# A message-passing layer on one core: the near products of a group run half by half instead of alternating

## What is computed

```python
h = jnp.maximum(_layernorm(x), 0.0)
l1_s, l1_v = fctp(x_s, x_v, lin1_ws, lin1_wv, MUL)       # per node
weight = silu(silu(rbf @ fc_w1) @ fc_w2) @ fc_w3          # per edge, from its distance
gs, gv = l1_s[edge_src], l1_v[edge_src]                   # gathered rows
msg = products of weight, gs, gv and edge_sh_attr         # 256 numbers per edge
agg = segment_sum(msg, edge_dst, N) / count               # sum per destination node
l2 = agg @ lin2_w
out = x + sc + tanh(agg_s @ alpha_w) * l2
```

## Time and profile before

| what | value |
|---|---|
| median of three runs | 3177.41 us |
| span of the profiled execution, first to last instruction | 3111.8 us |
| its own time outside the span | not recorded; the median is 65.6 us above the span |
| TensorE matmuls busy | 1998.8 us (64%) |
| VectorE busy | 1672.2 us (54%) |
| GpSimd busy | 1500.1 us (48%) |
| ScalarE busy | 1094.8 us (35%) |
| mean granted TensorE clock | 0.764 of full |
| near product, line 1052 | 3126 matmuls, 472.8 us busy |

### The profile page before, as it was taken

The page is one execution under the profiler, slowest core; times in us unless marked ns, Lnnn a source line. Parts: engine busy times, 40 slices in busy tenths (PEclk is TensorE's granted clock), DMA queues, the critical chain, the costliest instruction groups (busy, mean ns, idle before and its releaser), DMA issues. The chain is left out here.

```text
span 3111.8 us, 47493 instructions
## 1 busy us (share of the span) xinstructions
PE 1998.8 (64%) x9991; PEld 1344.9 (43%) x9991; DVE 1672.2 (54%) x4467; ACT 1094.8 (35%) x3268; POOL 1500.1 (48%) x1607
## 2 busy tenths in 40 slices
PE   6566566566766666656666666665666575656567
PEld 5344344344444444434344444443444443434444
DVE  7454555455554555545455455554554554556556
ACT  6333333333333334323333233332333232334334
POOL 6544445444544444544444544544545444544452
PEclk8687777788877778777777767777877777777778
DMA  7211111121212112111111111111111111222211
GB/s 205 49 45 42 45 40 44 42 47 39 51 39 45 41 43 47 40 38 36 39 35 39 39 36 39 39 39 37 40 34 42 35 38 38 45 58 59 47 41 46
DMA packets 329818, 143.39 MB, mean 46 GB/s; under 512 B 242675, under 2 KB 304428, under 8 KB 329628
## 3 DMA queue, kind: packets, MB, share of 16 engines
q0 software_dynamic: 49344, 101.13, 12.4%
q1 hardware_dynamic: 268038, 34.58, 7.3%
q10 hardware_dynamic: 12246, 6.06, 0.7%
HBM read 127.88 MB, written 13.75 MB: 46 GB/s over the span
## 5 line engine op out<-in xcount | busy, mean ns | idle before, releaser
L990 POOL DMA_INDIRECT lin_g<-lin_table,src_ix x1542 | 1459.6, 947 | 1557.7 <-DVE w_s L1417 1017.7
L1064 PE MATMUL ps_sums<-near_sums,far_hot 128*128 128x1 f32 x520 | 119.3, 299 | 917.9 <-DVE agg L1476 842.6
L1040 PE MATMUL ps_w<-w,h 128*128 128x256 f32 x1566 | 582.8, 528 | 115.7 <-ACT h L1157 69.8
L1476 DVE SCALAR_TENSOR_TENSOR agg<-ps_sums,at_lo,agg 128x130 f32 x260 | 91.4, 352 | 893.0 <-remote 775.8
L1064 PEld LDWEIGHTS ps_sums<-near_sums,far_hot 128*128 128x128 f32 x520 | 102.0, 245 | 1082.6 <-issue 764.5
L1176 ACT ACTIVATE near_sums<-ps_near 128x257 f32<-128x257 f32 x261 | 100.7, 386 | 1168.1 <-remote 826.9
L1040 PEld LDWEIGHTS ps_w<-w,h 128*128 128x128 f32 x1566 | 423.1, 298 | 177.7 <-issue 93.0
L1168 ACT ACTIVATE lin_sh<-lin_g,harm 128x128 f32<-128x128 f32 x1563 | 483.8, 393 | 36.4 <-DMA lin_g<-lin_table 27.5
L1052 PE MATMUL ps_near<-msg,onehot 128*64 128x257 f32 x3126 | 472.8, 445 | 0.0
L1414 DVE TENSOR_TENSOR msg<-lin_sh,ps_w 128x576 f32<-128x576 f32 (+1 forms) x261 | 196.1, 751 | 455.7 <-remote 191.2
L1052 PEld LDWEIGHTS ps_near<-msg,onehot 128*64 128x64 f32 x3126 | 235.8, 162 | 234.4 <-issue 178.0
(11 more groups left out here) (175 smaller groups left out, 1983.7 us busy)
## 6 DMA issues: line engine op xcount, KB each, us to landing
lin_g<-lin_table SPq DMA_DIRECT2D x2688, 0.5 KB
lin_g<-lin_table,src_ix POOLq DMA_INDIRECT x1542
dist_in<-in_edge_weight SPq DMA_DIRECT2D x67, 96.0 KB
lin_table<-lin_out SPq DMA_DIRECT2D x24, 256.0 KB, 3.0
x_in<-in_x SPq DMA_DIRECT2D x24, 256.0 KB
xq<-in_x SPq DMA_DIRECT2D x23, 256.0 KB, 4.1
harm<-in_edge_attr SPq DMA_DIRECT2D x66, 48.0 KB
out_dram<-x_in ACTq DMA_DIRECT2D x11, 256.0 KB
```

The lines of the kernel that those rows point to most:

```text
L990: pool.indirect_dma_start(slot_tiles(s, u)[rows, t, :], None, lin_table, bass.IndirectOffsetOnAxis(ap=src_ix[rows, s.phase, u, col:col + 1 ...
L1040: mm = pe.matmul(ps_w[:, 2 * j * P:(2 * j + 2) * P], cols[:, j, :], w3[:], start=True, stop=True)
L1064: pe.matmul(ps_l2(i)[:, COUNT:COLS], far_hot[:, u, :], near_sums[:, u % 2, MSG:], start=True, stop=True)
```

## The change

In `near_layer` the two loops are exchanged. Before, the products went 0, 1, 2, 3, 4, 5 by tile, that is first half, second half, first half and so on. After, tiles 0, 2, 4 (first half) come first, then 1, 3, 5. The same six products with the same operands are issued, and the increment stays on the last one, which is tile 5 in both orders.

```diff
                             at_least(pe, near_copied, n)
                             pe.nop(nofuse=True)
-                            for j in range(PAIRS):
-                                for half in range(1 if isinstance(i, int) and i == ITERS else HALVES):
+                            for half in range(1 if isinstance(i, int) and i == ITERS else HALVES):
+                                for j in range(PAIRS):
                                     t = j * HALVES + half
                                     mm = pe.matmul(ps_near[half * NEAR:(half + 1) * NEAR, 0:MSG + 1], onehot[:, u % 2, t, :], msg[:, u % 2, t, :],
                                                    start=(j == 0), stop=(j == PAIRS - 1))
```

## The result

The changed kernel took 3197.09 us, the median of six runs (3185.86 to 3202.32). The kernel before, whose three shown runs had a median of 3177.41, took 3169.72 over six runs (3161.8 to 3177.78). The ratio is 1.0082, with a 95% interval of 1.0053 to 1.011: **slower by 0.8%, 27 us**. The forecast was slower, by 90 us, at 3267 us. Direction and range (3163 to 3390) held; the size was over three times too large.

The account below looks back on a forecast made before the run. The bound was taken to be the cycle of gather bursts and held-back TensorE completions, not matmul work. Caught sums, 72 us, plus direct payments, 18 us, make 90 us on 3177.41: 3267 us, range 3163 to 3390.

Parts of the forecast that it names:

- The bound is a cycle of bursts and holds: GpSimd gathers in unbroken bursts; TensorE's completions are held from about 4 us in until after the end; one group 10.66 us.
- If three is also the most it can pass: In TensorE's near product the second half starts with the first half's fourth matmul: nine slots, 0.69 us longer.
- Rival 1: TensorE's second half passes the whole queue, both halves overlap from the start, time stays 3177 us; chance 0.36.
- rival 2: TensorE's matmuls start only in instruction order: eleven slots, five more, 1.15 us; 3352 us; chance 0.14.
- Most near products are covered by a hold: Most near products end inside a hold, so 0.69 us more still ends before the release and costs nothing.
- 2.17 us for each sum that is caught: A segment sum held until after a burst makes the cycle 12.83 us instead of 10.66; 33 of them, 72 us.
- 26 groups pay their 0.69 directly, 18 us: Where no hold lies behind the near product, its added 0.69 us is paid directly: 26 groups, 18 us.
- Rival 3: Delayed `ps_w` is caught in a hold, joined two-group bursts are split, 88 us less, 3089 us; chance 0.09.
- Rival 4: All of the near product's added time is on the path: 179 to 364 us, 3357 to 3541; chance 0.04.

Follow-up runs that it names:

- sets 4 and 5: Two groups of runs on the same chip, some five minutes apart; the kernel before took 3176.31 us in the first (with holds), 2016.42 in the second (without).
- e1: Kernel before with the near products ordered first, first, second, first, second, second half; 2015.23 us against 2015.03, ratio 0.9999, without holds.
- e7: Kernel before, alternating order, with layer 1 moved behind the segment sum; 3136.41 us, ratio 1.0042, with holds.
- e8: Changed kernel with layer 1 moved behind the segment sum; 3179.53 us, ratio 1.0192 to the kernel before, with holds.
- sets 2 and 4: Two groups of runs with holds, each beside the kernel before, which took 3120.95 us in the first and 3176.31 in the second.
- d1: Kernel before, alternating order, with one more product of 255 columns into an unused part of the bank; 3195.3 us, ratio 1.0057, with holds.
- d3: Kernel before with all rows gathered by GpSimd and SyncE's single-row DMAs left out; 3124.06 us, ratio 0.9832, with holds.
- c1: The changed kernel itself, unedited, run again beside the kernel before; 3133.72 us, ratio 1.0038, with holds.
- e3: Kernel before, alternating order, with two more products of 255 columns into an unused part of the bank; 3175.04 us, ratio 1.0173, with holds.
- d2: The changed kernel itself, run again beside the kernel before; 3197.52 us, ratio 1.0073, with holds.
- c2_half: The changed kernel itself, run again beside the kernel before, without holds; 2013.33 us, ratio 1.0.

## Why the prediction was right in direction and wrong in size

1. *The bound is a cycle of bursts and holds, not TensorE's amount of work.* Right where the holds are: TensorE stays idle 34% of the span with 0.48 us more in each near product. But the holds come and go with the same kernel, even on one chip (sets 4 and 5). Without holds the same kernel takes 2015 us and the bound is GpSimd's issuing of gathers.
2. *"If three is also the most it can pass", three slots more, 0.69 us.* Mis-sized: the second half starts one matmul earlier, two slots, 0.48 us (2.00 against 1.52), since TensorE passes at least five waiting instructions, not three. Rival 1 (no slot lost) and rival 2 (strict order, 2.7 us) both fall. The Trainium skill (TensorE: Matmul & The Clock Gate, Part 3, "The mechanism") has matmuls start and end in strict order; the traces disagree, with 2.00 us for this order and 1.57 us for that of e1, where strict order would need three slots more in either.
3. *Most near products are covered by a hold.* Right in what follows from it: of 260 x 0.48 = 125 us added, 13, 21 and 27 us were paid in the three comparisons with the kernel before, 10 to 22%, and 43 us, 34%, between e7 and e8. That it is the holds that cover the rest was read from single groups, not tested.
4. *"2.17 us for each sum that is caught", 33 more of them, 72 us.* **This is the step that failed.** Caught sums rose by 16 (by 10 and 14 in sets 2 and 4, against the same one profile of before), not 33, and 2.17 us for each does not give the times. The 16 alone would be 35 us, above all that was measured, 27, with the direct payments still to come. e7 should have gained about 20 us and lost 15, d1 (3 more caught) should have cost 7 us and cost 19, e8 (2 more) 4 and cost 59. e7 and e8 also slowed layer 1, so the plainest case is d1; d3 (19 fewer caught, 52 us less) is the one run that the price would fit. One cycle of 12.83 us against one of 10.66 was a true reading of one place, but one cycle is not the mean. Counted over the trace, such long cycles rose by 8, and cheap one-group cycles rose by 16 beside them.
5. *26 groups pay their 0.69 directly, 18 us.* This small term was the nearest to what is seen: the price follows the near product's added length. Within set 4, 0.43 us cost 19 us and 0.48 cost 21; in set 2 the 0.48 us of c1 cost 13 and the 0.85 of e3 cost 54. That is 17%, 17%, 10% and 24% of the length added over 260 groups, so the share isn't constant, and with more length it seems to grow. With the 0.48 us measured, a tenth of the groups makes 12 us, a fifth 25.
6. *Rival 3, bursts are split.* It is there (165 waits for `w_s` instead of 147, 157 in d2) and did not win. The two-group cycles also became longer by 0.5 us each, which eats what the splits give.
7. *Rival 4, all on the path.* It falls at every bound tried; the most was paid in the one-gather kernels, 0.20 of 0.48 us.

Why a tenth to a third is paid with holds, and no more, stays **open**. The clock is no large part of it: the mean granted clock rose from 0.764 to 0.783 with the change, but of the 113.5 us that the near product's busy time gained (line 1052, 472.8 to 586.3), TensorE's other work gave back only 5 (1998.8 to 2107.4 in all). That the pattern of joined and single bursts shifts, some groups losing and others gaining, is argued from the counts above and was not shown by a run. No version tried that computes the same beats both kernels in both conditions: e1 equals the kernel before (tried without holds only, where a longer product costs nothing either), e7 is slower, and d3's gather by GpSimd alone gives 1.7% with holds and loses 1.3% without.

## What to carry to other kernels

Issue small products that use different column halves of the array in turn, with at most two in a row into the same half: two in a row made the near product 0.05 us longer here, three 0.48 us. When a stretch that is not the bound gets longer, ask what share of its groups ends in no other wait, and price that share by the added length; do not multiply the one striking cycle that you found by all the places where it could occur. And compare effects of 1% by several interleaved runs: one profiled execution was 1.8% off its own median.

## What the runs showed of the hardware

- TensorE starts an instruction for free columns ahead of those that wait for busy ones, past five of them and, by the starts of the loads in e1, six (e1: 1.57 us, the changed kernel: 2.00 us for the same twelve matmuls), not past seven.
- The same kernel takes 2013 to 2016 us in some sets of runs and 3121 to 3176 in others. In the former the profiles show no wait for results held back, and TensorE's mean granted clock is 0.92 in the kernel before; in the latter it is 0.77. The condition with holds costs over a third of the time, far more than anything that the change touches. It is not fixed to a chip (sets 4 and 5), and the holds don't depend on SyncE's single-row DMAs (d3). Whether long runs of gathers make them was not tried where they occur.
- The place of a short product in TensorE's order sets its clock: layer 1 took 0.91 us ahead of a long wait and 1.64 us just behind one of 9.79 us (e7).
- A kernel with a busy share of 92% on TensorE took 0.5 us more per group for nothing (`c2_half`): even there the gathers of GpSimd, busy 74% of the span and issuing for most of the rest (463 us), were the bound.
